# Decoder layer on one core: row-maximum pieces over three engines, one query copy, residual additions on VectorE, new call lists

## The reference, cut to what matters

```python
x = x + attention(layernorm(x), Wq, Wk, Wv, Wo)               # T=128, 16 heads of 16
x = x + convolution(ctx, ctx, layernorm(x), ssm_kernel, D, 8)  # layernorm(x) is the query
x = x + ffn(layernorm(x), gate, up, down)                      # 4-bit codes, 2048 wide

# attention: masked scores are multiplied by the mask, not set to minus infinity
scores = einsum(q, k) * tril(ones(T, T))
out = softmax(scores / T ** 0.5) @ v
# convolution: kv[i, j] = k[i] * v[j] in each group of 8, convolved along the tokens
# with ssm_kernel, plus kv * D; then out[j] = sum over i of conv(kv)[i, j] * q[i]
# ffn: gelu(x @ gate) * (x @ up) @ down
```

## Time and profile before

| What | Value |
|---|---|
| Median of 3 runs | 260.15 us |
| The profiled execution's own time | 259.66 us |
| Its span in the trace | 257.9 us |
| Instructions | 5025 |
| TensorE clock granted, whole span | 0.996 of full speed |
| DMA, mean over the span | 73 GB/s |

### The profile page before, as it was taken

How to read it: one execution, slowest core, us unless ns; L and a number is a source line. 1 busy time by engine, 2 the same in 40 slices (tenths; PEclk the granted TensorE clock), 3 DMA queues, 4 the chain that set the end, 5 groups by cost and what they waited for, 6 DMA issues and landing times.

```text
span 257.9 us, 5025 instructions
## 1 busy us (share of the span) xinstructions
PE 243.8 (95%) x1872; PEld 158.3 (61%) x1872; DVE 149.8 (58%) x272; ACT 128.9 (50%) x281; POOL 153.2 (59%) x196
## 2 busy tenths in 40 slices
PE   7999999999998899887999999999999999999993
PEld 7855766566666567564446677566566566566562
DVE  3878668784896889889457724327145182322124
ACT  3354665478775777765656434315333343523230
POOL 4268455785129799998999964183453635432230
PEclk9999999999999999999999999999999999999998
DMA  7995996940240003100012000003030000000004
GB/s 229 364 344 165 150 240 187 175 124 0 97 155 1 4 0 93 40 0 0 1 31 94 3 0 0 3 1 122 3 104 18 3 1 0 0 3 0 0 3 163
DMA packets 15104, 18.81 MB, mean 73 GB/s; under 512 B 1448, under 2 KB 12776, under 8 KB 15080
## 3 DMA queue, kind: packets, MB, share of 16 engines
q1 hardware_dynamic: 15080, 18.49, 26.1%
HBM read 15.21 MB, written 3.15 MB: 71 GB/s over the span
## 4 chain that ended last, share of the span: by engine, by line
PE 84%; DVE 6%; ACT 5%; issue 2%; POOL 1%; DVEq 0%; ACTq 0%; POOLq 0%
PE bank L1230 38%; PE bank L1396 16%; PE bank L1286 4%; PE bank L1288 3%; PE bank L1209 3%; PE bank L1284 3%; PE bank L1302 3%; PE bank L1470 2%; ACT PT L616 2%; PE bank L1468 1%; PE bank L1421 1%; PE bank L1354 1%; DVE o_sb L986 1%; PE bank L1423 1%; PE bank L1338 1%
## 5 line engine op out<-in xcount | busy, mean ns | idle before, releaser
L466 POOL TENSOR_TENSOR QK<-QK 128x512 f16<-128x512 f32 x31 | 35.8, 1157 | 54.7 <-ACT QK L645 54.5
L1035 DVE SCALAR_TENSOR_TENSOR QK<-bank,QK 128x512 f32<-128x512 f32 x32 | 22.1, 691 | 63.6 <-PE bank L1230 60.2
L655 ACT ACTIVATE QK<-bank 128x512 f32<-128x512 f32 x32 | 19.0, 596 | 59.9 <-PE bank L1230 59.8
L1230 PE MATMUL bank<-xTh,Wb 128*128 128x512 f16 x128 | 40.7, 379 | 0.0
L1230 PE MATMUL bank<-xTh,Wa 128*128 128x512 f16 x128 | 40.4, 379 | 0.0
L442 POOL TENSOR_TENSOR arena<-Ys,qx 128x640 f32<-128x640 f32 x16 | 26.7, 1672 | 3.5 <-ACT qx L707 3.5
L1230 PE MATMUL bank<-xTl,Wb 128*128 128x512 f16 x64 | 24.3, 379 | 0.0
L1230 PE MATMUL bank<-xTl,Wa 128*128 128x512 f16 x64 | 24.3, 379 | 0.0
L969 DVE TENSOR_REDUCE mx<-bank 128x8 f32<-128x1024 f32 x16 | 19.5, 1218 | 7.7 <-PE bank L1319 7.7
L1396 PE MATMUL bank<-Wa,QK 128*128 128x256 f16 x192 | 23.4, 273 | 0.0
L1396 PE MATMUL bank<-Wb,QK 128*128 128x256 f16 x192 | 23.3, 273 | 0.0
(11 more groups left out here) (149 smaller groups left out, 495.5 us busy)
## 6 DMA issues: line engine op xcount, KB each, us to landing
arena<-in_codes SPq DMA_DIRECT2D x6, 384.0 KB
arena<-in_ker SPq DMA_DIRECT2D x2, 1024.0 KB, 12.1
QK<-qk_scratch SPq DMA_DIRECT2D x8, 256.0 KB, 5.9
arena<-in_ctx SPq DMA_DIRECT2D x2, 768.0 KB, 7.6
qk_scratch<-Wa SPq DMA_DIRECT2D x12, 128.0 KB, 3.0
arena<-in_gu_scale SPq DMA_DIRECT2D x6, 256.0 KB
QK<-qk_scratch SPq DMA_DIRECT2D x8, 128.0 KB, 5.8
out<-XN SPq DMA_DIRECT2D x4, 256.0 KB, 2.4
```

The costliest lines, as they stand in the source:

```text
L466: g_.tensor_tensor(il[:, u % IR], val[:, u % VR], ih[:, u % IR], ALU.subtract).then_inc(s_il, 1)
L655: s_.activation(val[:, u % VR], bank[2 * (u % 2)][:, :], ACT.Gelu_apprx_tanh, scale=1.0 / W_GAIN).then_inc(s_gel, 1)
L1035: v_.scalar_tensor_tensor(out=val[:, u % VR], in0=bank[2 * (u % 2) + 1][:, :], scalar=UP_SCALE, in1=val[:, u % VR], op0=ALU.mult, op1=ALU. ...
L1230: ins = mmul(out, a(c), w(c), start=(n == 0), stop=(n == 3 * len(chunks) - 1))
```

## The change

It has six parts.

1. **Row maxima.** The scaling with the guard goes from GpSimd to VectorE, behind the second `pair_max` of a batch. The f16 high part is made by ScalarE from `ms` (`max_hi`, which now calls `exp_max`), and the low part stays on GpSimd.
2. **Query.** `take_query` fills the 16-wide field with one copy that repeats the eight values; `conv_products` reads other offsets of it.
3. **Codes.** `codes_join` masks the signs inside the instruction that joins (a `scalar_tensor_tensor`), five instructions in place of six.
4. **Residual of the attention.** No identity matmul in `project_out`; `take_out` is gone, and `stats_cross` begins with a VectorE addition of the bank to X.
5. **Residual of the cross step.** No identity matmul in `add_cross`, R is transposed, `take_cross` is gone, and `stats_ffn` begins with a VectorE addition.
6. **Call lists** of all five engines in a new order.

```diff
             def max_pieces(b):
-                pool.wait_ge(s_max, 2 * b + 2)
...
+                pool.wait_ge(s_mhi, b + 1)
-                g_.tensor_scalar(ms[:, r], mx[:, r], guard[:, 0:1], 1.0 / MAX_GAIN, ALU.max, ALU.mult).then_inc(s_ms, 1)
-                g_.tensor_scalar(hi, view(mx[:, r], by_half), guard[:, 0:1], 1.0 / MAX_GAIN,
-                                 ALU.max, ALU.mult).then_inc(s_ms, 1)
                 g_.tensor_tensor(lo, view(ms[:, r], by_half), hi, ALU.subtract).then_inc(s_mch, 1)
...
+            def max_hi(b):
+                sc.wait_ge(s_ms, b + 1)
+                if b >= 2:
+                    sc.wait_ge(s_mpt, b - 1)
+                s_.activation(view(mp[:, b % 2], [[16, 2], [4, 2], [1, 4]]),
+                              view(ms[:, b % 2], [[4, 2], [8, 2], [1, 4]]), ACT.Copy).then_inc(s_mhi, 1)
+                exp_max(b)
...
+                if p == 1:
+                    ve.wait_ge(s_max, n + 1)
...
+                    v_.tensor_scalar(ms[:, b % 2], mx[:, b % 2], guard[:, 0:1], 1.0 / MAX_GAIN,
+                                     ALU.max, ALU.mult).then_inc(s_ms, 1)
...
-                s_.activation(view(qx[:, b % 2], [[16, 2 * H], [1, HD]], 4),
-                              view(bank[6][:, :], [[HD, 2 * H], [1, HD]]),
-                              ACT.Copy).then_inc(s_qx, 1)
-                s_.activation(view(qx[:, b % 2], [[16, 2 * H], [12, 2], [1, 4]]),
-                              view(bank[6][:, :], [[HD, 2 * H], [-4, 2], [1, 4]], 4),
-                              ACT.Copy).then_inc(s_qx, 1)
+                s_.activation(view(qx[:, b % 2], [[16, 2 * H], [HD, 2], [1, HD]]),
+                              view(bank[6][:, :], [[HD, 2 * H], [0, 2], [1, HD]]),
+                              ACT.Copy).then_inc(s_qx, 1)
...
-                v_.tensor_scalar(t[:, 576:768], t[:, 576:768], -0x7F7F7F80, None, ALU.bitwise_and).then_inc(s_bits, 1)
-                v_.tensor_tensor(bits(j), t[:, 0:384], t[:, 384:768], ALU.bitwise_or).then_inc(s_bits, 1)
+                v_.scalar_tensor_tensor(out=bits(j), in0=t[:, 0:384], scalar=-0x7F7F7F80, in1=t[:, 384:768],
+                                        op0=ALU.bitwise_and, op1=ALU.bitwise_or).then_inc(s_bits, 1)
...
             def stats_ffn(b):
+                ve.wait_ge(s_rt, b + 1)
+                v_.tensor_tensor(X[:, b, :], X[:, b, :], bank[6][:, 0:D], ALU.add).then_inc(s_x2, 1)
                 ve.wait_ge(s_x2, b + 1)
                 ln_stats(2, b)
...
             def stats_cross(b):
+                ve.wait_ge(s_proj, b + 1)
+                v_.tensor_tensor(X[:, b, :], X[:, b, :], bank[7][:, 0:D], ALU.add).then_inc(s_x1, 1)
                 ve.wait_ge(s_x1, b + 1)
                 ln_stats(1, b)
...
             def add_cross(b):
-                mmul(bank[6][:, 0:D], ident[:, :], X[:, b, :], start=True, stop=False, skip_group_check=True)
-                    last = mmul(bank[6][:, P * c:P * c + P],
-                                R[:, b % 2, H * c:H * c + H, :].rearrange("p h i -> p (h i)"),
-                                ident[:, :], start=False, stop=(c == 1), skip_group_check=True)
+                    last = t_.transpose(bank[6][:, P * c:P * c + P],
+                                        R[:, b % 2, H * c:H * c + H, :].rearrange("p h i -> p (h i)"), ident[:, :])
...
             def project_out(b):
-                mmul(bank[7][:, 0:D], ident[:, :], X[:, b, :], start=True, stop=False)
-                    last = mmul(bank[7][:, 0:D], oT[:, b % 2, c, :], wo[:, c, :], start=False, stop=(c == 1))
+                    last = mmul(bank[7][:, 0:D], oT[:, b % 2, c, :], wo[:, c, :], start=(c == 0), stop=(c == 1))
```

More of the change, by code:

```diff
@@ L500, in _ @@
             conv_products(0, 0)
-            conv_products(0, 1)
-            rstd_cross(1)
             decode_scale(2, 0)
             max_pieces(5)
+            rstd_cross(1)
+            conv_products(0, 1)
+            rstd_cross(2)
             decode_scale(2, 1)
-            max_pieces(6)
-            rstd_cross(2)
             conv_products(1, 0)
             conv_products(1, 1)
+            max_pieces(6)
             max_pieces(7)
@@ L527, in _ @@
             rstd_cross(7)
+            conv_products(6, 0)
+            conv_products(6, 1)
+            act_lo(0)
             decode_scale(3, 0)
-            conv_products(6, 0)
             decode_scale(3, 1)
-            act_lo(0)
-            conv_products(6, 1)
             act_lo(1)
@@ L536, in _ @@
             conv_products(7, 0)
+            act_lo(2)
             conv_products(7, 1)
-            act_lo(2)
             act_lo(3)
@@ L737, in _ @@
             conv_out(7, 1)
+            max_hi(0)
             conv_out(8, 0)
@@ L1122, in _ @@
             sum_slots(0, 0)
-            sum_slots(0, 1)
             pair_max(6, 0)
@@ L1126, in _ @@
             pair_max(6, 1)
+            sum_slots(0, 1)
             normalise(3)
@@ L1541, in _ @@
             project_out(0)
-            attend(2, 0)
-            row_scores(4, 1)
             turn_values(1)
@@ L1546, in _ @@
             row_scores(5, 0)
+            attend(2, 0)
             attend(2, 1)
+            attend(2, 2)
+            turn_heads(1)
+            attend(2, 3)
+            project_out(1)
             key_scores(3, 0)
-            turn_heads(1)
-            attend(2, 2)
-            attend(2, 3)
             turn_query(0)
+            row_scores(5, 1)
+            turn_values(2)
+            attend(3, 0)
             key_scores(3, 1)
-            attend(3, 0)
-            project_out(1)
-            turn_values(2)
+            turn_max(4)
             attend(3, 1)
-            turn_max(4)
-            row_scores(5, 1)
             attend(3, 2)
@@ L1562, in _ @@
             turn_heads(2)
+            row_scores(6, 0)
             project_out(2)
-            row_scores(6, 0)
             key_scores(4, 0)
+            row_scores(6, 1)
+            key_scores(4, 1)
+            turn_max(5)
+            attend(4, 0)
+            row_scores(7, 0)
             turn_values(3)
-            key_scores(4, 1)
-            row_scores(6, 1)
-            attend(4, 0)
-            turn_max(5)
+            turn_query(1)
             attend(4, 1)
             attend(4, 2)
+            key_scores(5, 0)
+            add_cross(0)
+            turn_heads(3)
             attend(4, 3)
-            row_scores(7, 0)
-            turn_query(1)
-            turn_heads(3)
-            add_cross(0)
-            key_scores(5, 0)
+            turn_query(2)
+            attend(5, 0)
             row_scores(7, 1)
+            key_scores(5, 1)
             project_out(3)
-            key_scores(5, 1)
-            turn_query(2)
+            attend(5, 1)
             turn_max(6)
+            turn_max(7)
             turn_values(4)
-            turn_max(7)
-            attend(5, 0)
-            attend(5, 1)
             attend(5, 2)
+            turn_ffn(0)
             add_cross(1)
-            turn_ffn(0)
+            key_scores(6, 0)
             attend(5, 3)
-            key_scores(6, 0)
+            attend(6, 0)
+            turn_heads(4)
             turn_values(5)
-            turn_heads(4)
             key_scores(6, 1)
+            attend(6, 1)
+            turn_query(3)
+            key_scores(7, 0)
             project_out(4)
-            turn_query(3)
-            attend(6, 0)
-            key_scores(7, 0)
-            attend(6, 1)
+            key_scores(7, 1)
             attend(6, 2)
+            attend(6, 3)
             turn_heads(5)
-            attend(6, 3)
             attend(7, 0)
-            attend(7, 1)
             turn_ffn(1)
             add_cross(2)
-            key_scores(7, 1)
-            turn_values(6)
-            project_out(5)
-            turn_query(4)
+            attend(7, 1)
             attend(7, 2)
             attend(7, 3)
+            turn_values(6)
+            turn_query(4)
+            project_out(5)
+            turn_heads(6)
             turn_values(7)
-            turn_heads(6)
+            add_cross(3)
             turn_ffn(2)
-            add_cross(3)
             project_out(6)
@@ L1641, in _ @@
             down(2)
+            turn_ffn(5)
             down(3)
```

281 lines of the change are left out of this document (132 added, 149 removed).

## The result

The changed kernel takes **263.74 us**, the median of 20 runs (259.86 to 266.4), against 260.15 us before (259.83 to 260.68, 20 runs). The ratio is 1.008, 95% interval 1.0064 to 1.0097. That ratio leaves out runs more than 1.5% above the fastest one, and here these are half of the 20, so the medians tell more: 3.6 us, 1.4%, slower. Forecast were 256.6 us and a range of 253.0 to 260.0. Not only is the middle of the runs higher; the runs of the kernel before lie within 0.9 us and those of the changed one within 6.5.

What follows compares the result with a forecast made beforehand. TensorE was taken to bound most stages, with three engines sharing the bound in the middle. 259.66 - 1.8 (middle) - 0.8 (its start) - 1.0 (fourth window) = 256.1 us profiled, 256.6 as median; range 253.0 to 260.0.

Steps and rivals of the forecast that it cites:

- What TensorE loses: project_out and add_cross: matmuls dropped or replaced by transposes, 8.6 us less full TensorE time as ceiling, 6.0 in the middle.
- What VectorE gets: Middle, 66.40 to 124.50 us: list from 50.9 to 53.3 us, by +5.4 additions, +1.4 ms, -4.4 moved off.
- What VectorE waits: Middle: waits fall from 7.2 to 3.0 us (between 1 and 7.2), so the stage takes 56.3 against 58.1, -1.8.
- The start of the middle: Before 65.06 us: maxima fill VectorE's 3.85 us wait for TensorE; start moves by -0.8 us, between 0 and -1.5.
- The fourth window: 124.50 to 157.10 us: GpSimd sets it, -0.9 to -1.7 us, taken as -1.0.
- SyncE's order: SyncE's list, small max_rows DMAs and loads of codes: costed at nothing, the codes being needed tens of microseconds later.
- The clock: A granted clock below 1.00 in a stage where TensorE idles, named as a sign of a wrong forecast, without size.
- C: Middle: VectorE becomes the bound and keeps 7.2 us of waiting on a list of 53.3; 260.9 us, chance 0.13.
- B: Lists fit well: VectorE waits 1 us in the middle, start -1.5, fourth window -1.7; 253.2 us, chance 0.23.
- D: TensorE time saved lies in calls that waited anyway; middle stays, fourth window gives 1.0; 259.1 us, chance 0.14.
- the change doesn't do what it says: Fourth window: transposes of R as long as the matmuls would give back 0.6 us; no chance of its own.

Runs made afterwards that it cites:

- e5: Changed kernel plus 22 small identity matmuls into an unused bank where TensorE waits, 112 to 126 us: 260.02 us median, before 259.95.
- e8: Changed kernel with SyncE's old list, loads of codes behind the rows' DMAs as before: 262.75 us median, before 259.95.
- e2: Kernel before with the residual additions alone (parts 4 and 5), old lists, no fillers: 259.51 us median, before 260.02.
- e6: Kernel before with parts 4 and 5 alone, old lists, plus 25 filler matmuls where TensorE waits: 258.71 us median, before 259.95.
- e9: All five edits in the old lists, plus 25 filler matmuls where TensorE waits: 259.37 us median, before 260.22.
- e10: e6 with the cross step's residual on VectorE for batches 4 to 7 only, 0 to 3 as before: 257.53 us median, before 260.22.
- e11: Kernel before with only the cross step's residual of batches 4 to 7 on VectorE, no fillers: 258.39 us median, before 260.22.
- the good case: The changed kernel's first profiled execution, the fastest of its 20 runs: 259.86 us.
- e12: The changed kernel run again unchanged, as control: 262.52 us median of 6 runs, before 260.22; its profiled execution took 263.16 us.
- e1: Kernel before with parts 1 to 3 alone, lists in the old order: 260.42 us median, before 260.02.
- e4: Changed kernel with an overwritten f32 identity matmul put back in project_out and add_cross: 263.21 us median, before 260.02.

## Why the prediction was wrong, step by step

- **What TensorE loses: right in size, wrong in worth.** 8.6 us were forecast and the busy time fell by 6.8; part of what is left ran at 1.2 GHz and so counts longer. In e5, at a clock of 1.000, it is 240.8 with 5.3 us of fillers (22 of 0.24), which makes 8.3 less than before. The fourth window kept its share of it; the middle did not.
- **What VectorE gets: right.** I forecast a list of 53.3 us for the middle. It measured 59.6 less 6.0 of waits (the waits by line, less the 0.87 before the first `tail`), 53.6. An addition takes 408 to 416 ns; none was stretched. `ms` takes 255 ns.
- **What VectorE waits: this is the step that failed first.** Forecast 3.0 us, measured 6.0, and 5.2 in e5 at full clock. The step said "the rest shrinks because a fuller list reaches each wait later". With the new lists it did not: the waits for `turn_values` and `project_out` are 5.3 of the 6.0, while TensorE, with less to do, waits in turn for `tail`, `xTl` and X. I had treated the other engines' times as given; they wait for each other. One piece has a cause that a run shows, the rows of `max_rows(3)` behind the loads of codes (e8); for the rest the ring is read from the waits, and no run takes it apart. With the old lists the waits did shrink, to 2.3 us, and VectorE ran at 92% (e2), but that list is longer by as much, and unit 0 starts no earlier: 124.89 against 124.75. So -1.8 us became +1.6 with the new lists (+0.9 in e5, at full clock), and about 0 with the old.
- **The start of the middle: wrong.** Forecast -0.8, measured -0.1 (66.34 against 66.48; 66.57 in e5). TensorE does the calls ahead of `turn_values(0)` in another order, but nearly as many of them, and `tail` still waits 0.87 for it.
- **The fourth window: the number near, the mechanism wrong.** Forecast -1.0, with "GpSimd sets it"; 126.17 to 157.32 is 31.2 us against 32.4, -1.2. But TensorE sets it: in e6, e9, e10 and e11 the stretch is 30.4, -2.0, the 1.95 us that TensorE no longer does, without a wait. With the new lists that is less 0.22 for `add_cross(4)` and 0.35 for one wait, and 0.2 stay unexplained. That it came out near -1.0 is luck, and it holds only for the good case: in e12 the stretch is 33.1, +0.8, since the clock is at 1.2 GHz as it begins.
- **SyncE's order: at nothing, wrong.** I wrote that the loads of codes are needed tens of microseconds later. They are, but `max_rows(3)` stands behind them: `key_scores(3, 0)` waits 0.30 us for its rows in the good case, 0.79 in e5 and 1.12 in e12, and 0 in e8.
- **The clock: not in the sum.** I named a clock below 1.00 in a stage where TensorE idles as what would make the forecast wrong, and gave it no price and no chance. It is worth 2.2 us (e5 against e12) to 3.5 (against the first 20 runs), and 1.8 by the ratios. Of the 3.6 us by which unit 8 starts later in e12 than in e5 (160.61 against 157.06), 1.6 lie ahead of unit 0 and 2.0 behind it.
- **The rivals.** C had the place and the mechanism (VectorE as the bound of the middle, TensorE held by it), the sign, and 0.13; its price was +0.7, e5 at full clock is at +0.1, and what made 263.7 of it is the clock. The Trainium skill's rule, in Perfetto Trace Analysis, Optimizing Scalar/DVE Operations, that work may go from a saturated VectorE to ScalarE, is borne out in part: e10 takes four additions back off VectorE and gains 1.2 us, of which the traces leave 0.46 to it. B, D and the case that the change doesn't do what it says did not occur, though D's reading of the middle, that the time saved lay in calls that waited anyway, is what e2 and e11 show.

Put together, at a nearly full clock: parts 1 to 3 cost 0.4 (e1; e9 against e6), the additions gain 1.2 (e6), the new order costs 0.9 (e5 against e9), which leaves about 0; the clock then takes 2.2 to 3.5. Step by step in e5: the start is 0.1 later where I took 0.8 off, the middle 0.9 longer where I took 1.8 off, and the stretch behind it 1.2 shorter where I took 1.0 off. That is 3.4 of the some 3.6 us by which the sum was too low at full clock; the clock added 2.2 to 3.5 more.

Left open: the rest of what the new order costs. The traces show two places, the rows behind the loads of codes and the wait before an `add_cross`; neither was tried at a steady clock, and the other moves were not tried one by one.

## What to carry to other kernels

Work taken off the fullest engine is worth its time only in the stages where that engine has no waits: cut the profile into stages first, and make the edit only where it pays (e11 changes four batches of eight and gains 1.8 us, the whole change lost 3.6). In a stage that several engines share, price the engine that receives the work, and take its waits as unchanged or growing, not as cover. A short DMA that something waits for should not stand behind long loads in the list that issues it. When TensorE will wait more ahead of a stage that is full of matmuls, look at the granted clock of every run and not of one profile, and put matmuls that compute nothing into the waits.

## What the runs showed of the hardware that was not expected

The granted clock fell in a stage in which TensorE was never idle for long. In the changed kernel its longest wait in the 15 us ahead was the 2.14 us before 119.11, with waits of 0.5 to 0.9 us around it, and the clock was 0.60 from 120 to 124 us; in e2 it was 0.50 at 126 to 128 us, when TensorE was already busy for the whole two microseconds. In e12, with a longest wait of 2.22 us, it was still 0.50 from 128 to 130. The same kernel, run again, lost between 0.8% and 3.2% of its clock, so one profile does not show it. The Trainium skill, page TensorE: Matmul & The Clock Gate, section A second HAM failure mode: psum-queue depth-cycling, tells of a kernel whose frequent small pauses between groups of matmuls make the clock go to and fro between its two levels; these traces agree, with pauses of 0.5 to 2.1 us.

Fillers of 0.24 us each (1.95 us for eight), 22 of them in pauses ahead of unit 0, brought the clock back to 0.999 or 1.0 in 7 runs of 12 and cost nothing that can be seen: unit 0 starts at 125.92 with them and at 126.17 in the good case without. Identity matmuls in front of the calls themselves (e4) also brought it back, and that kernel took 3.1 us more than e5.

The twelve additions of the middle, with one input in a PSUM bank, take 0.40 to 0.42 us each, and none was stretched, where the product `o_sb`, with both inputs in SBUF, once took 1.70.
